# Split products for the queries and the cross output of a decoder layer, eight batches of rows held instead of sixteen

## The reference

```python
# attention: 16 heads of 128, one shared key/value head, window 128, partial rope, a sink logit
q = h @ wq_comp @ wq_up
q = _rmsnorm(_apply_partial_rope(q, cos, sin), q_norm_w)
k = _rmsnorm(_apply_partial_rope(h @ wk, cos, sin), k_norm_w)
probs = jax.nn.softmax(jnp.concatenate([scores, sink], axis=-1), axis=-1)
x = jnp.einsum('btgi,gio->btgo', x, out_w1).reshape(b, t, G * INTER)
return x @ out_w2
...
# cross attention: 16 heads of 32, causal against the context
out = jnp.einsum('bhqk,bhkd->bhqd', attn, vh)
return out @ Wout.T
...
# feed-forward: 4 of 32 experts for each token, plus a shared expert
```

## Time and profile before

| | us |
|---|---|
| median of 3 runs (lowest, highest) | 1190.68 (1186.55, 1194.47) |
| profiled execution, its own time | 1187.81 |
| its span, first to last instruction | 1185.9 |
| busy: PE, DVE, ACT, POOL | 1141.3, 811.3, 594.3, 344.8 |
| mean granted clock of TensorE | 0.989 |

### The profile page before, as it was taken

The page is one execution under the profiler, slowest core; times in us unless marked ns, Lnnn a source line. Parts: engine busy times, 40 slices in busy tenths (PEclk is TensorE's granted clock), DMA queues, the critical chain, the costliest instruction groups (busy, mean ns, idle before and its releaser), DMA issues. The chain is left out here.

```text
span 1185.9 us, 21051 instructions
## 1 busy us (share of the span) xinstructions
PE 1141.3 (96%) x7761; PEld 901.9 (76%) x7762; DVE 811.3 (68%) x1392; ACT 594.3 (50%) x1404; POOL 344.8 (29%) x279
## 2 busy tenths in 40 slices
PE   6989999999999999999999989999999999999995
PEld 3457677777767777776777666887889999999994
DVE  1255797889789878978987886643266666666662
ACT  1334554565455446545544644421146666666662
POOL 0011103211311221131123112222046666666643
PEclk9999999999999999999999989999999999999998
DMA  8450000000000000000000005042089999999974
GB/s 279 143 175 19 1 9 10 14 16 2 16 14 9 9 14 16 8 10 14 9 9 16 14 10 204 9 163 80 28 293 264 258 261 280 269 274 271 271 148 54
DMA packets 62598, 117.59 MB, mean 99 GB/s; under 512 B 10932, under 2 KB 14564, under 8 KB 62388
## 3 DMA queue, kind: packets, MB, share of 16 engines
q1 hardware_dynamic: 44820, 82.46, 20.6%
q0 software_dynamic: 17728, 34.44, 14.6%
HBM read 93.55 MB, written 28.13 MB: 103 GB/s over the span
## 5 line engine op out<-in xcount | busy, mean ns | idle before, releaser
L1503 POOL TENSOR_TENSOR rall<-qkv_var,phalf 100x17 f32<-100x17 f32 x16 | 49.1, 3071 | 404.4 <-DVE qkv_var L1177 404.4
L391 PE MATMUL QS<-xh,wh 128*128 128x256 f32 x512 | 147.2, 288 | 0.0
L392 PE MATMUL QS<-xl,wh 128*128 128x256 f32 x512 | 144.8, 283 | 0.0
L393 PE MATMUL QS<-xh,wl 128*128 128x256 f32 x512 | 144.8, 283 | 0.0
L1581 POOL DMA_INDIRECT out_rows<-work,idx x64 | 106.1, 1658 | 101.3 <-DMA out_rows<-work,idx 47.1
L391 PE MATMUL W<-wch,oth 128*100 128x512 f32 x256 | 105.1, 410 | 0.0
L392 PE MATMUL W<-wcl,oth 128*100 128x512 f32 x256 | 100.6, 393 | 0.0
L393 PE MATMUL W<-wch,otl 128*100 128x512 f32 x256 | 100.4, 392 | 0.0
L392 PEld LDWEIGHTS QS<-xl,wh 128*128 128x128 f32 x512 | 98.2, 192 | 1.2
L391 PEld LDWEIGHTS QS<-xh,wh 128*128 128x128 f32 x512 | 98.0, 191 | 1.2
L393 PEld LDWEIGHTS QS<-xh,wl 128*128 128x128 f32 x512 | 98.1, 192 | 0.0
(11 more groups left out here) (225 smaller groups left out, 2863.3 us busy)
## 6 DMA issues: line engine op xcount, KB each, us to landing
raw<-in_w SPq DMA_DIRECT2D x24, 1024.0 KB
raw<-in_w SPq DMA_DIRECT2D x24, 512.0 KB
work<-in_w SPq DMA_DIRECT2D x8, 1024.0 KB
work<-in_w SPq DMA_DIRECT2D x8, 512.0 KB
hx_rows<-h3x SPq DMA_DIRECT2D x16, 212.5 KB
h_columns<-h3s SPq DMA_DIRECT2D x16, 200.0 KB, 1.9
h3T<-h_columns SPq DMA_DIRECT2D x4, 800.0 KB, 15.2
out_rows<-ytiles POOLq DMA_DIRECT2D x14, 200.0 KB, 2.5
```

Source lines behind the costliest of these rows:

```text
L391: mm(dst, ah, bh, start=start, stop=False)
L392: mm(dst, ah, bl, start=False, stop=False)
L393: return mm(dst, al, bh, start=False, stop=stop)
L1503: return nc.gpsimd.tensor_tensor(out=dst, in0=src, in1=phalf[:, 0:src.shape[1]], op=ALU.pow)
```

## The change

Five edits:

1. **Queries** of batches 2 to 15 become split products. ACT writes `hqh` in place of `hqT` (the same copy, rounded), DVE writes `hql` (128x100, `queries_low`) after the sum L1307 of the step, and PE waits for it (`hq_low`). Batches 0 and 1 stay fp32.
2. **Cross output** becomes split products for all batches. ACT writes `oxh` in place of `oxT`, DVE writes `oxl` (128x400, `values_low`) after `routed` and ahead of L1334, and PE's ranks and cross output wait for it (`ox_low`). In the pipeline it goes into `qb[3]`, a bank of the scores, instead of `wb[3]`; so the wait for `cross_added` moves from the fourth group of query transposes to the fourth bank of scores.
3. **Order.** PE transposes the cross probabilities straight after the router, then heads 12 and 13, the cross values, heads 14 and 15. DVE rotates the keys behind the queries. ACT takes the router's exponential after the four copies of transposed cross probabilities.
4. **Rows.** Only eight batches of rows are held. In steps 2 to 9, SP stores the finished row c = b - 2 to device memory, waits for it, and loads batch c + 8 in its place; the eight stored rows come back in two loads of four for the shared expert's sums. DVE's steps 7, 8 and 9 are written out.
5. **Weights.** The halves of `w_up` and `w_out` are made once: two ACT copies at the end of step 0, two DVE subtractions at the end of step 0 and in step 1.

```diff
             def queries(c):
+                whole = isinstance(c, int) and c < WHOLE
                 pe.wait_ge(s.hqT, c + 1)
+                if not whole:
+                    pe.wait_ge(s.hq_low, c - WHOLE + 1)
...
+                        last = split_product(qb[i][0:T, :], hqh[:, :], hql[:, :], w_uph[:, w], w_upl[:, w], True, True)
...
-            def cross_out(b):
-                pe.wait_ge(s.oxT, b)
+            def cross_out(b, bank):
+                pe.wait_ge(s.ox_low, b)
...
+                    last = split_product(bank[0:T, :], oxh[:, c], oxl[:, c], w_outh[:, w], w_outl[:, w], k == 0, k == KC - 1)
...
-                        if i == 3 and do.C:
-                            pe.wait_ge(s.x2, b - 1)
...
                         pe.wait_ge(s.qT, 4 * b + i + 1)
+                        if i == 3 and do.C:
+                            pe.wait_ge(s.x2, b - 1)
...
                     router(b - 2)
-                if do.A:
-                    project(b, range(12, 14))
...
                     cross_transposed(qb)
                 if do.A:
-                    project(b, range(14, 15))
+                    project(b, range(12, 14))
...
-                    project(b, range(15, 16)).then_inc(s.x1_ps, 1)
+                    project(b, range(14, 16)).then_inc(s.x1_ps, 1)
...
-                        pe.wait_ge(s.oxT, b)
+                        pe.wait_ge(s.ox_low, b)
                     ranks(b - 2)
                 if do.X:
-                    cross_out(b)
+                    pe.wait_ge(s.pxT, 4 * b)
+                    cross_out(b, qb[3])
...
+            def queries_low(c):
+                dve.wait_ge(s.hqT, c + 1)
+                dve.wait_ge(s.q_ps, 4 * c)
+                tt(hql[:, :], wb[1][:, 0:T], hqh[:, :].bitcast(fp32), ALU.subtract).then_inc(s.hq_low, 1)
+            def values_low(b):
+                dve.wait_ge(s.oxT, b)
+                dve.wait_ge(s.x2_ps, b - 1)
+                tt(oxl[:, :], wb[1][:, 0:QW], oxh[:, :].bitcast(fp32), ALU.subtract).then_inc(s.ox_low, 1)
...
                     red(den[:, :], P3, AX.X, ALU.add).then_inc(s.p_sum, 1)
+                    if do.Q and not (isinstance(b, int) and b + 1 < WHOLE):
+                        queries_low(b + 1)
...
+            def row_swapped(c):
+                sp.wait_ge(s.ln3_base, c + 1)
+                sp.dma_start(based[:, bass.ds(c, 1), :], rv[:, bass.ds(c, 1), :]).then_inc(s.row_st, 16)
+                sp.wait_ge(s.row_st, 48 + 16 * (c + 1))
+                sp.wait_ge(s.ld_x, 16 * (c + 1))
+                sp.dma_start(rv[:, bass.ds(c, 1), :], xv[:, bass.ds(c + HELD, 1), :]).then_inc(s.ld_x, 16)
...
             sp.wait_ge(s.x2_ps, NB)
+            sp.wait_ge(s.ld_x, 16 * (HELD + 2))
+            sp.dma_start(back[0:T, 4 * HID:8 * HID].rearrange("t (b d) -> t b d", d=HID), based[:, 4:8, :]).then_inc(s.ld_x, 16)
```

More of the change, by code:

```diff
@@ L134, in build @@
         oxT, h3s, h1T, h2T, qpT, ckT = (sb(n, [P, 400]) for n in ("oxT", "h3s", "h1T", "h2T", "qpT", "ckT"))
-        hqT, kT, ctxT = (sb(n, [P, T]) for n in ("hqT", "kT", "ctxT"))
+        kT, ctxT = (sb(n, [P, T]) for n in ("kT", "ctxT"))
+        hqT = place("hqT", [P, T], fp32, oxT_at)
+        oxh = place("oxh", [P, QW], f32r, oxT_at)
         kvs_at = used[0]
@@ L160, in build @@
         cv, normw = (sb(n, [T, HID]) for n in ("cv", "normw"))
+        hqh, hql = sb("hqh", [P, T], f32r), sb("hql", [P, T], f32r)
+        oxl = sb("oxl", [P, QW], f32r)
         at = WX + 4 * HXW
@@ L235, in build @@
         table = nc.dram_tensor("expert_lists", [NE * CAP, 1], i32, kind="Internal").ap()
+        based = nc.dram_tensor("base_rows", [T, NB - HELD, HID], fp32, kind="Internal").ap()
         h3d = nc.dram_tensor("h3_columns", [P, NB, KC * T], fp32, kind="Internal").ap()
-        half = [[t[:, 0:2048], t[:, 2048:4096]] for t in (w_x, resid[:, HID * NB // 2:HID * NB])]
+        half = [[t[:, 0:2048], t[:, 2048:4096]] for t in (w_x, odd)]
         block = ctx.enter_context(nc.Block())
@@ L324, in step @@
                     sp.dma_start(dst, h3x[:, :]).then_inc(s.hx_st, 16)
-            pipeline(sp, step)
+                if swap:
+                    row_swapped(b - 2)
+            step(0)
+            step(1)
+            with sp.Fori(2, HELD + 2) as b:
+                step(b, True)
+            with sp.Fori(HELD + 2, NB - 1) as b:
+                step(b)
+            sp.wait_ge(s.q_ps, 4 * NB)
+            sp.wait_ge(s.ld_x, 16 * (HELD + 1))
+            sp.dma_start(back[0:T, 0:4 * HID].rearrange("t (b d) -> t b d", d=HID), based[:, 0:4, :]).then_inc(s.ld_x, 16)
+            step(NB - 1)
             def load_columns(g, done):
@@ L824, in compressed @@
                 act.wait_ge(s.q_ps, 4 * c)
-                copy(hqT[:, :], banks[1][:, 0:T]).then_inc(s.hqT, 1)
+                whole = isinstance(c, int) and c < WHOLE
+                copy((hqT if whole else hqh)[:, :], banks[1][:, 0:T]).then_inc(s.hqT, 1)
                 act.wait_ge(s.kv_ps, c + 1)
@@ L929, in step @@
                     squares(b + 1)
-                if do.C:
-                    act.wait_ge(s.topd, b - 1)
-                    act.wait_ge(s.top_w, 2 * (b - 2))
-                    fn(e4[:, :], d4[:, :], ACT.Exp, accum_out=sum4[:, :]).then_inc(s.top_exp, 1)
+                if first:
+                    copy(w_uph[:, :], w_up[:, :]).then_inc(s.high, 1)
+                    act.wait_ge(s.ld_wx, 64)
+                    copy(w_outh[:, :], w_out).then_inc(s.high, 1)
                 if do.X:
@@ L1021, in _ @@
             act.wait_ge(s.oxT_ps, NB)
-            copy(oxT[:, :], wb[1][:, 0:QW]).then_inc(s.oxT, 1)
+            copy(oxh[:, :], wb[1][:, 0:QW]).then_inc(s.oxT, 1)
             shared_inner(3)
@@ L1259, in ranked, with cross_added @@
                 nc.vector.tensor_copy(tok[:, :], tokall[:, bass.ds(c, 1)]).then_inc(s.slots, 1)
-            def cross_added(c):
+            def cross_added(c, bank=qb[3]):
                 dve.wait_ge(s.x2_ps, c + 1)
-                tt(row(c), row(c), wb[3][0:T, :], ALU.add).then_inc(s.x2, 1)
+                tt(row(c), row(c), bank[0:T, :], ALU.add).then_inc(s.x2, 1)
                 wait_alone(dve, s.x2, c + 1)
@@ L1325, in step @@
                     rotate(b + 1)
+                if do.Q:
+                    rotate_keys(b + 1)
                 if do.X:
                     cross_normed(b)
+                if isinstance(b, int) and b == 1:
+                    out_weights_low()
                 if do.Q:
@@ L1349, in step @@
                     cross_added(b - 1)
+                if isinstance(b, int) and b == 0:
+                    up_weights_low()
             wait_alone(dve, s.ld_x0, 16)
@@ L1362, in _ @@
             joined(range(13, 14))
-            pipeline(dve, step)
+            step(0)
+            step(1)
+            with dve.Fori(2, HELD - 1) as b:
+                step(b)
+            for b in range(HELD - 1, HELD + 2):
+                step(b)
+            again[0] = 1
+            with dve.Fori(HELD + 2, NB - 1) as b:
+                step(b)
+            step(NB - 1)
             def split_low(n):
```

102 lines of the change are left out of this document (66 added, 36 removed).

## The result

The changed kernel's median is 1188.24 us over 20 runs (1182.80 to 1204.42), that of the kernel before over the 20 runs beside them 1193.95 us (1186.55 to 1211.33; the three runs shown ahead of the prediction had given 1190.68). The ratio is 0.9955, with a 95% interval of 0.994 to 0.997: faster by 0.45%, some 5.4 us. Forecast were 9.4 us and 1181; the sign is right, the time lies in the range, and the gain is a little over half of the one forecast. The ratios are of fast runs alone; the profiles of experiments 7 and 9 are of slow ones (1208.22 and 1213.57 us), whose loop steps are as regular as those of the others.

What follows compares the result with a forecast made beforehand. PE was taken as the bound, with DVE's stretch closed over PE next at 40.70 us. 9.1 + 0.9 + 0.9 + 0.7 - 2.2 = 9.4 us off, so 1181 against 1190.7; range 1168 to 1189.

Steps and rivals of the forecast that it cites:

- second return load: Ahead of the experts' weights on SP's queue: 0.82 MB at 341 GB/s adds backlog; +2.2 us, bounds 0 and 4.
- step 15 and the last cross output: End of the pipeline: earlier scores and a lost stall save 0.9 us, the last cross output 0.7.
- the 8.00 us wait: DVE's wait in the shared expert, read as a 200 KB store of sums standing behind SP's backlog.
- The two rings: Pipeline step: PE's own list, and DVE's stretch closed over PE; the latter sets the new period, 40.70, near 40.75 us.
- rival a: Pipeline: PE alone binds, so its full 1.74 us a step counts; 24.7 us gained, time 1166; chance 0.16.
- DVE's stretch: From the attention add to the end of the cross probabilities' division, without waits for PE: 35.06 us, plus 0.20 for `hql`.
- both arrive together: At the cross-probability transposes: from `hql`'s end PE needs some 16.5 us, DVE 16.5 to the division's end.
- Queries 0.60 on PE and cross output 0.66: PE, each step: split products take 2.83 us each instead of 3.43 and 3.49, saving 0.60 and 0.66.
- `oxl` in front of the add: DVE ahead of the attention add: its 0.63 us fits into the wait for PE, with 0.46 us of cover.
- Rival (c): DVE: late `oxl` delays the attention add and PE's next step; +0.9 us a step, time 1203; chance 0.08.
- The written-out steps: DVE's three written-out steps lack the 0.30 us pause at the loop's edge; -0.9 us, 0 if code loading takes it.
- rival (b): Pipeline: small margins fail and half a microsecond a step goes; 2.4 us gained, time 1188; chance 0.18.

Runs made afterwards that it cites:

- experiment 7: Changed kernel with the cross output as one fp32 product again, no low part on DVE; ratio to the kernel before 0.9975.
- experiment 9: Changed kernel with queries and cross output both whole fp32 products again, other edits kept; ratio to the kernel before 1.0025.
- experiment 6: Changed kernel with all queries as one fp32 product again, no low part on DVE; ratio to the kernel before 0.996.
- experiment 10: Changed kernel with the low part of the cross values computed three times on DVE; ratio to the kernel before 1.0034.
- experiment 8: Changed kernel with PE's old order of heads, router's exponential ahead of ACT's copies, second return load issued earlier; ratio to the kernel before 0.9923.
- experiment 1: Changed kernel with PE's old order: heads 12 and 13 ahead of the transposes, head 14 ahead of the cross values; ratio to the kernel before 0.9997.
- experiment 4: Changed kernel with the second return load issued ahead of the last turn of the sums; ratio to the kernel before 0.9933.
- experiment 3: Changed kernel with PE's old order of heads and the queries' low part made earlier; ratio to the kernel before 1.0051.
- experiment 11: Changed kernel with the queries' low part made earlier and the second return load issued earlier; ratio to the kernel before 0.9894, median 1178.41 us.
- experiment 5: Kernel before, unchanged, profiled a second time; 1195.45 us in the profiled execution, median 1194.21 us.
- experiment 2: Changed kernel with `hqh` copied ahead of the cross scores and `hql` made ahead of DVE's sum; ratio to the kernel before 0.9964.

## Why the prediction was right or wrong

**In short.** The mechanism in the loop was right. The sum had four terms too favourable: the second return load was put at +2.2 and cost 4.2; step 15 and the last cross output were put at 1.6 and gave 0.65; the steps ahead of step 3 were put at 1.3 and gave 0.4; and the twelve steps from 3 to 15 were put at 8.7 and gave 7.85. The largest is the load. The step that failed there is the one from bytes to time, 0.82 MB at 341 GB/s making 2.4 us, together with the reading that the 8.00 us wait is a store lying behind SP's backlog.

**Against which profile.** Set beside the second profile of the kernel before (1193.4 us of span), which has the clock's lows where the changed kernel's has them, the ledger closes: step 15's POOL instruction is 8.27 us earlier (680.61 to 672.34); the last add ahead of the store's wait 8.92 earlier (798.17 to 789.25); the shared expert's last such add only 4.71 earlier (827.42 to 822.71); the end 5.2 (1193.4 to 1188.2). The sum of the prediction was 9.4. So 1.73 are missing in the steps (10.0 forecast), 0.95 between them and the wait (1.6 forecast, 0.65 measured), and the wait took 4.2 in place of 2.2. With a rest of 0.5 the other way in what comes after, these are the 4.2 that are missing. (That both the load's cost and the missing sum are 4.2 is a coincidence.)

**The two rings: right.** The period was forecast near 40.75 and is 40.80; PE alone (rival a, 39.65) doesn't bind, as PE's 0.71 us wait for `hql` shows (near 1 forecast). The ring was put together as 35.26 (DVE's stretch with `hql` in it) + 0.06 + 5.38 = 40.70, and measured 35.07 + 0.25 + 5.48 = 40.80. Its sum came out within 0.1 partly by luck, for two of its parts were off and cancel. The step from the division to the transposes is 0.25 us in the changed kernel and in experiments 6, 9 and 10, not 0.06. And the stretch is 35.07, not the 35.3 that I had named as a sign: `hql` lengthens it by 0.05 (35.02 without it in experiment 6) and not by 0.20, as it starts before the sum's end (329.85 against 329.93), which the next instruction has to wait for anyway. That "both arrive together" at the transposes was read as a coincidence that costs nothing. It is a second ring, with `hql` in it (18.65 + 0.14 + 22.01, experiment 8), and it is why neither experiment 1 nor 8 gained from the old order, whose shorter way from the transposes to the attention add (4.30 against 5.48) would have freed 1.2 us of DVE's ring.

**The parts.** Queries 0.60 on PE and cross output 0.66: right as durations (2.83 each), worth little in the period: 0.39 together, and either alone gives it all. `oxl` in front of the add: 0.55 us of wait left (about 0.5 forecast), and the cover ends where it should (experiment 10). Rival (c)'s mechanism sets in with the old order (by under 0.1 us) and with the low part made three times, but the changed order keeps clear of it. Keys and query transposes: no stall, and the 16 transposes take 1.53 (1.54 forecast). Rows held: hidden, as a loop step with a row stored and loaded takes as long as one without (40.80 from step 6 to 7, 40.82 from 13 to 14).

**The written-out steps: right** in size: 0.87 in all, 0.9 forecast.

**Steps 1 and 2, step 15 and after: too much.** I counted 14 steps at 0.65 from step 1 on; the twelve from step 3 to step 15 gave 496.94 - 489.09 = 7.85 (the first of them, from step 3 to 4, only 0.26: 41.39 to 41.13), the first ones 0.42 together. There DVE's subtraction for the halves of `w_out` takes 2.29 us (143.32), and step 2's POOL instruction is 2.23 later (145.77 against 143.54), but step 3's is 0.42 earlier again; why these steps didn't give their 1.3 stays open. In step 15 PE waits 4.66 us for DVE in both kernels, so what PE saves ahead of it is not gained there.

**The second return load: the term that was mis-sized most.** Forecast +2.2 with bounds of 0 and 4; measured +4.2. That the load is the cause is shown by experiment 4, which moves it alone and takes 3.3 of the wait away. How it costs so much is in POOL's list. POOL issues the stores of the sums, and it first waits until its own scattered writes have landed. POOL's and DVE's timelines of the second profile of the kernel before, then of the changed kernel:
```profile
803.24 1.16 POOL L1556 DMA_DIRECT2D h1T<-expert_lists  x2 [4.75 <-DMA expert_lists<-tok,slot]
804.35 1.15 POOL L1563 DMA_DIRECT2D out_rows<-ytiles  x2
806.98 0.69 DVE L1397 TENSOR_TENSOR ytiles<-resid,W 100x512 f32<-100x512 f32 x1 [8.13 <-DMA out_rows<-ytiles]
```
```profile
795.43 1.16 POOL L1651 DMA_DIRECT2D h1T<-expert_lists  x2 [5.85 <-DMA expert_lists<-tok,slot]
796.54 1.14 POOL L1658 DMA_DIRECT2D out_rows<-ytiles  x2
```
In the kernel before DVE's last add starts at 798.17, the stores are issued 6.18 us later and DVE goes on 2.63 after that: most of the 8 us is no store lying in a queue but a store not yet issued, and when it is, SP's queue has run dry (0.00 MB from 803 to 804 us). So the prediction misread. In the changed kernel the same pieces are 7.29 (789.25 to 796.54) and 5.31 (to 801.85), and from there to the last add 20.86 in place of 20.44: 1.11 + 2.68 + 0.42 = 4.21. With the load early (experiment 4) they are 6.63, 2.64 and 20.50, together 0.52 over the kernel before.

The price wasn't 2.4 us of queue. Windows of the return load: the second profile of the kernel before, where there is none; the changed kernel, at the same place; experiment 4, where it runs with only small transfers beside it:
```profile
793.00:799.00 6.00, 6.00 (x28) 4.25 (x27) 1.43 (x3) 0.00 (x0) 3.97 (x4) 1.00 1.02 390
786.00:792.00 6.00, 6.00 (x27) 4.25 (x26) 1.38 (x2) 0.00 (x0) 2.94 (x3) 1.00 1.04 241
763.00:769.00 6.00, 6.00 (x35) 6.00 (x34) 4.03 (x7) 3.73 (x3) 4.94 (x4) 1.00 0.54 136
```
By itself the load takes about 6 us, and among the weights the DMA engines are fully busy but move 241 GB/s in place of 390. SP's queue takes some 18.5 us from the issue of `h3T` (781.61) until it runs dry, in place of 12.5.

An earlier arrival isn't what lengthens the wait. Experiment 3 comes to it when the kernel before does (last add at 798.42 and 798.17) and waits 12.90 us; the runs with the load early wait 8.40 to 8.58 though they come 8.7 to 17.6 us sooner. And PE's 5.31 us of idleness is followed by a longer low of the clock: 0.50 and 0.76 in the two windows shown above, where the first profile of the kernel before has 0.57 and 1.00.

By the rule of the Trainium skill, "DMA: Bandwidth & Descriptors", section on queues, rings and completion order, each DMA engine takes turns between queues packet by packet, so a small store doesn't sit out another queue's backlog. The trace agrees. DMA queues of the changed kernel from 798 to 799 us (q0 is POOL's, q1 SP's; packets, MB, share):
```profile
q1 hardware_dynamic: 128, 0.25, 65.7%
q0 software_dynamic: 40, 0.07, 25.0%
```
Both move at once, and the store takes 5.31 us beside SP's packets where it takes 2.63 alone. But the prediction's reading of the rule, that the term would then be 0, isn't borne out either: sharing the engines made the store slower.

**The basis.** 1181 was 9.4 below the median of three runs, 1190.7; the medians of the later sets of 20 to 34 runs lie at 1193.8 to 1194.5. That has no part in the gain, but the ratio, not the time, is what the steps are to be held against; 1188.2 lies inside the range that ended at 1189 by 0.8 us.

**Chances.** The measured case is one that had 0.60 (within 1%); between the forecast's own range (5 to 14 us) and rival (b)'s 2.4 us the result lies at the lower edge of the forecast, though not by (b)'s mechanism: the margins held.

## What to carry to other kernels

In a software pipeline an engine's gain counts only as far as the next ring: close every ring through the engines, the instruction that is newly waited for included, and add a real handover time (0.25 us here) to each change of engine, before pricing a shorter product. Two edits that shorten the same list needn't add: here either split product gave all that both give. Split a wait for a store at the moment when the store is issued, and look what the issuing engine waited for: here over half of it lay before that. And price a load put ahead of others by how long one like it holds the DMA engines (about 6 us for 0.8 MB here), not by its bytes over the rate of the big loads (2.4); moving it to an idle stretch of the queue was worth two fifths of what the steps had gained (3.5 of 8.3 us).

## What was unexpected of the hardware

The same wait, with the same idle time of PE, is followed by a lower clock in some executions and not in others. Window from 69 to 76 us of experiment 11's profile (idle 3.07 us just before):
```profile
69.00:76.00 7.00, 7.00 (x58) 5.88 (x59) 3.56 (x5) 2.04 (x6) 0.56 (x1) 1.00 0.23 83
```
That is 2.4 GHz throughout, where the second profile of the kernel before shows 0.52 after 2.96 us of idleness. By step 3 the two executions of the kernel before are 6.0 us apart (1.2 of it from before this wait), as much as the whole change is worth; their mean granted clocks are 0.989 and 0.982. What decides it is open: the changed kernel's profile and those of experiments 4, 5, 7 and 10 have the low in full, 2 and 3 in part, and 1, 6, 8, 9 and 11 have none, which follows no edit. In the shared expert the clock fell after idle times of 5.31 (changed kernel), 2.55 (experiment 4: 0.65 from 804 to 808) and 1.93 us (kernel before, first profile: 0.57 there), and did not after 2.36 (experiment 11: 1.00 from 792 to 800). The idle time alone tells neither place.

The return load of 0.8 MB is slow for its size: 136 GB/s at a DMA share of 0.54 by itself, and 241 GB/s at a share of 1.04 among the weights, which alone reach 390. No run here shows why.
